# A fused decoder layer: scores ahead of turns in TensorE's order

## What is computed

```python
scores = jnp.einsum('bhsd,bhkd->bhsk', q, k) * scale
probs = jax.nn.softmax(scores, axis=-1)
out = jnp.einsum('bhsk,bhkd->bhsd', probs, v)
```

## Time and profile before

| | before |
|---|---|
| median of three runs | 735.23 us |
| profiled execution | 738.52 us |
| its span, first to last instruction | 736.8 us |
| TensorE matmuls, busy | 636.2 us (86%) |
| ScalarE busy | 415.1 us (56%) |
| VectorE busy | 407.7 us (55%) |
| GpSimd busy | 322.4 us (44%) |
| mean granted TensorE clock | 0.959 |

### The profile page before, as it was taken

The page is one execution under the profiler, slowest core; times in us unless marked ns, Lnnn a source line. Parts: engine busy times, 40 slices in busy tenths (PEclk is TensorE's granted clock), DMA queues, the critical chain, the costliest instruction groups (busy, mean ns, idle before and its releaser), DMA issues.

```text
span 736.8 us, 14686 instructions
## 1 busy us (share of the span) xinstructions
PE 636.2 (86%) x5168; PEld 511.4 (69%) x5168; DVE 407.7 (55%) x1113; ACT 415.1 (56%) x1498; POOL 322.4 (44%) x367
## 2 busy tenths in 40 slices
PE   3465899999999999999999999999998965299893
PEld 1245788887897888788878977887886752255552
DVE  1545555765865585767567655856443424145552
ACT  1222777676776775677667667766765631044441
POOL 4453343464266427444753574263324322234453
PEclk9998899999999999999999999999997995689998
DMA  7210000000000001001000000000000040223330
GB/s 153 65 32 26 1 1 3 22 5 2 1 26 30 1 1 56 1 3 26 29 2 2 1 30 2 1 22 10 1 1 29 30 154 33 92 82 97 96 95 14
DMA packets 25127, 23.60 MB, mean 32 GB/s; under 512 B 7055, under 2 KB 22673, under 8 KB 25056
## 3 DMA queue, kind: packets, MB, share of 16 engines
q1 hardware_dynamic: 21088, 15.83, 7.6%
q0 software_dynamic: 2816, 6.32, 2.4%
q10 hardware_dynamic: 1152, 0.52, 0.6%
HBM read 15.16 MB, written 8.02 MB: 31 GB/s over the span
## 4 chain that ended last, share of the span: by engine, by line
PE 57%; POOL 13%; DVE 9%; issue 8%; ACT 6%; DMA 5%; SPq 1%; POOLq 0%; DVEq 0%
PE bank L1052 7%; PE bank L1082 6%; PE bank L1073 5%; PE bank L1087 5%; PE bank L1062 5%; POOL routed L473 4%; PE bank L1015 4%; PE bank L1160 4%; PE bank L1088 4%; PE bank L1089 4%; ACT prob L863 4%; PE bank L958 2%; POOL prob L481 2%; PE bank L947 2%; DVE mneg L701 2%
## 5 line engine op out<-in xcount | busy, mean ns | idle before, releaser
L863 ACT ACTIVATE prob<-bank,mneg 128x128 f32<-128x128 f32 x512 | 182.5, 380 | 103.8 <-DVE mneg L701 103.8
L481 POOL TENSOR_TENSOR prob<-prob,rden 128x512 f32<-128x512 f32 x128 | 130.7, 1042 | 171.8 <-DVE rden L708 171.8
L863 ACT ACTIVATION_READ_ACCUMULATOR prob<-bank,mneg 128x1 f32 x512 | 111.8, 218 | 0.0
L869 ACT COPY probT<-bank 128x512 f32<-128x512 f32 x128 | 77.6, 606 | 47.7 <-PE bank L1062 46.7
L701 DVE TENSOR_REDUCE mneg<-bank 128x4 f32<-128x512 f32 x128 | 81.3, 678 | 32.1 <-PE bank L1052 32.1
L1052 PE MATMUL bank<-kT,qT 64*128 64x128 f32 x1024 | 76.2, 289 | 11.8 <-ACT kT L879 8.6
L1052 PEld LDWEIGHTS bank<-kT,qT 64*128 64x128 f32 x1024 | 64.0, 191 | 23.5 <-issue 18.0
L1062 PE MATMUL bank<-ident,prob 128*128 128x128 f32 x512 | 78.4, 276 | 0.0
L1073 PE MATMUL bank<-probT,V 128*64 128x128 f32 x1024 | 70.4, 280 | 1.4 <-ACT probT L869 1.4
L1062 PEld LDWEIGHTS bank<-ident,prob 128*128 128x128 f32 x512 | 60.7, 142 | 14.8 <-issue 13.5
L1082 PE MATMUL bank<-xwo,oT 128*128 128x128 f32 x512 | 64.8, 281 | 2.2 <-ACT oT L873 2.2
(11 more groups left out here) (165 smaller groups left out, 1335.2 us busy)
## 6 DMA issues: line engine op xcount, KB each, us to landing
prob<-routed SPq DMA_DIRECT2D x40, 128.5 KB, 2.1
xin<-in_x_dram SPq DMA_DIRECT2D x8, 256.0 KB, 3.0
ctx_nat<-in_ctx_dram SPq DMA_DIRECT2D x8, 192.0 KB, 2.5
routed<-blank SPq DMA_DIRECT2D x9, 128.5 KB, 2.2
qT<-in_L_ffn_rt_gate_dram SPq DMA_DIRECT2D x1, 1024.0 KB, 5.3
qT<-in_L_ffn_rt_up_dram SPq DMA_DIRECT2D x1, 1024.0 KB, 9.0
out_dram<-probT,prob POOLq DMA_INDIRECT x40
prob<-in_L_xattn_Wq_dram SPq DMA_DIRECT2D x1, 512.0 KB, 11.6
```

The costliest lines, as they stand in the source:

```text
L481: nc.gpsimd.tensor_tensor(view, view, spread(rden[:, m % 2, c * NC:(c + 1) * NC], 2, S), ALU.mult)\
L863: last = nc.scalar.activation(prob[:, m % 2, p * S:(p + 1) * S], bank[c % 2][:, i * S:(i + 1) * S], ACT.Exp, bias=mneg[:, m % 2, p:p + 1], ...
L869: nc.scalar.copy(probT[:, m % 2, c * 512:(c + 1) * 512], made(r1, ("T", m, c))[:])\
```

## The change

In the steps `n` that have both batch `n` and batch `n + 1`, and in the even beats, the next batch's `scores` are issued ahead of this batch's `turn_probs` instead of behind them. That is so in 62 beats (31 steps, two beats each). The odd beats, and the order on all other engines, are as they were; the waits of each piece move with it.

```diff
@@ -1119,10 +1119,11 @@
             pe.wait_ge(consts, CONSTS_FIRST)
             for n in range(FIRST, LAST + 1):
                 for b in range(NC):
+
+                    if b % 2 == 0 and live(n + 1):
+                        scores(n + 1, b // 2)
                     if live(n):
                         turn_probs(n, b)
-                    if b % 2 == 0 and live(n + 1):
-                        scores(n + 1, b // 2)
                     if b % 2 and live(n + 1):
                         make_v(n + 1, b // 2)
                     if qk_of(n, b):
```

## The result

| | before | after |
|---|---|---|
| median beside the first comparison | 735.09 us (4 runs) | 742.9 us (4 runs) |
| profiled execution | 738.52 us | 740.88 us |
| TensorE's wait ahead of the scores | 11.8 us | 23.5 us |
| period of four batches, mid-loop | 68.2 us | 69.0 us |

The ratio is 1.0101 (95% interval 1.0072 to 1.013). A second comparison, with five rounds, gave 742.24 against 736.93 us, ratio 1.0077 (1.005 to 1.0104). So the kernel became slower by 5 to 8 us, and both medians lie inside the range given; the forecast of 744.2 lies 1.3 and 2.0 us above the two medians.

What follows compares the result with a forecast made beforehand. TensorE was taken as the bound. Losses of 3.6 us where it already waits (edge place included) and 5.4 us in covered beats make 9.0 us, moving the median from 735.2 to 744.2 us; range 738 to 750.

Steps and rivals of the forecast that it cites:

- waits of today: Where TensorE already waits for ScalarE before scores, turns no longer fill the wait: seven places lose 0.45 us each, 3.15 us.
- covered beats: Each period's first and third even beats, where turns hide ScalarE's lateness: 0.6 and 0.30 us lost, 5.4 us over six periods.
- the beat behind the sigmoids: ScalarE reloads the exponential's table; its copy of turns comes 0.54 us late, of which 0.3 us reaches the next scores.
- The one on the edge: At 513 us turns just cover ScalarE's exponentials; the scores would start at 513.66 instead of 513.19, losing 0.47 us.
- The fifth beat: Fifth even beat of a period: the 0.45 us lost before the scores comes out of the later wait for `h`.
- Usual beats: Even beats where ScalarE is done before the turns start: same 1.62 us sum, exponentials gain 0.04 us, counted as nothing.
- Only the waits of today pay: Rival: the twelve covered beats' margins of 0.27 to 0.33 us close, so they lose nothing; 739 us, chance 0.13.
- no change: Rival: every delay falls into a later wait, as in the fifth beats; 735.5 us, chance 0.11.
- faster: Rival: earlier scores hasten the row maximum if ScalarE's copy starts under about 0.25 us behind the turns; 732 us, chance 0.05.
- the rival of the clock: Rival: TensorE's longer single waits of 1.4 us also lower its granted clock, costing 5 to 10 us; 751 us, chance 0.13.
- the 3.3 us between profile and median: Profiled execution lies 3.3 us above the runs' median; carried over, so 747.5 us profiled means a median of 744.2.
- the rule that was weighed in the prediction: Changing the tiling mode drains TensorE; one more change in the loop's last four even beats, 0.08 us each, 0.3 us, left out.

Runs made afterwards that it cites:

- the fourth experiment: Scores ahead of turns only in the 13 beats where TensorE already waited ahead of the scores, against the kernel before: 737.65 us, ratio 1.003.
- the second experiment: Scores ahead of turns only in each period's first and third even beats, against the kernel before: 738.83 us, ratio 1.005.
- first experiment: Kernel before with the swap only in 23 even beats where ScalarE is done well before the turns: 734.28 us, ratio 0.9978; again 734.79 us, ratio 0.9994.
- exponentials first: Changed kernel, with ScalarE's exponentials of the next batch ahead of its copy of the turns in even beats: 760.31 us, ratio 1.0326.
- keys on VectorE, old order: Kernel before, with the last copy of the keys of each pair of batches made by VectorE instead of ScalarE: 735.29 us, ratio 1.0001.
- more beats with room: Kernel before with the first experiment's swaps plus halves 5, 6, 55, 57, 59, 61 and, unintended, 54 and 62: 737.62 us, ratio 1.0001.
- room only: Kernel before with scores ahead of turns in 29 beats, as in more beats with room but without halves 54 and 62: 734.04 us, ratio 0.9984.
- chosen version: Kernel before with the last keys' copy on VectorE and the swap only in each period's first, second, fourth, sixth and seventh half: 733.74 us, ratio 0.9972.
- new order, keys on VectorE: Changed kernel, with the last copy of the keys of each pair of batches made by VectorE: 737.73 us, ratio 1.0021.
- all but the sigmoid beat: Changed kernel with the old order in each period's eighth half, where ScalarE reloads the exponential's table: 740.3 us, ratio 1.0064.

## Why the prediction was right

- **The bound and what moves.** Swaps with room cost nothing, swaps without it cost what the turns had covered, and one swap made ScalarE late for the beat behind it. The traces add up. From the scores of half 1 to the product behind half 53, at full granted clock in every profile from 81 to 555 us, the changed kernel took 5.92 us more than the one before (433.34 against 427.42). The parts, each against the same stretch: 1.67 us (waits of today) + 2.76 (covered beats) + 2.34 (the beat behind the sigmoids, 5.92 - 3.58) - 0.92 (beats with room) = 5.85 us. The medians of the whole kernels give 2.2 + 3.4 + 1.9 to 2.6 - 0.6 to 1.2 = 6.3 to 7.6 us against 5 to 8, but each of these terms is uncertain by more than 1 us, and six swapped beats are in none of the parts.
- **Waits of today.** Each was to cost 0.45 us and cost 0.37 to 0.41 in the places up to 542 us, measured from the row ahead of the two pieces to the product behind them. Turns between the other pieces hold TensorE 0.41 us, not 0.45, and ScalarE's exponentials start 2.27 us behind the scores, not 2.36, since its instructions overlap by 0.1. The first three beats cost 1.16 us instead of 1.35: by the trace the scores of half 5 start 0.71 us later against those of half 0, and they should start 0.45 sooner. The last two places, at 557 and 578 us, cost 0.57 and 0.60: there `prob_v` stands behind the turns (last section). The one on the edge, at 513 us, cost 0.40 (forecast 0.47).
- **The fifth beat.** Given back at `h`, as worked out; shown by the fourth experiment.
- **The covered beats.** The third cost 0.33 us (forecast 0.30), the first 0.69 to 0.70 (0.6), of which the sigmoid beat's lateness made 0.44. Both terms were a little small.
- **Usual beats.** I had counted them as nothing; each saves 0.02 to 0.08 us, 0.2 in a period. The period grew by 0.8 us, since the covered beats took 1.0 and these gave 0.2 back: the forecast of 0.9 is that close partly because two errors cancel.
- **The rivals.** "Only the waits of today pay" fell with the second experiment, "no change" with the period, "faster" with the copy at 0.69 us behind the turns. The granted clock stayed at full from 77 to 610 us in the profile of the changed kernel, with waits of 1.40 us in it, and in its second profile too, so the rival of the clock is not borne out there.
- **Profile against median.** Here the mechanism had a hole. The forecast took the stretch at the lower clock around 565 us as unchanged, and put the profiled execution at 747.5 us; it took 740.9. Neither profile of the changed kernel has that stretch. From the product behind half 53 to that behind half 63 the kernel before took 78.8 us; the kernel with only the covered beats swapped, which has the old order there and was granted the full clock, took 74.6; the changed kernel took 76.2. So at equal clock the changed kernel is 5.9 + 1.6 = 7.5 us longer, and against the profile of before only 5.9 - 2.6 = 3.3 us. The two medians' differences, 7.8 and 5.3 us, lie between these or next to them; what share of the runs without a profile has the stretch is not known. That the median came within 2 us of 744.2, while the profiled execution missed by 6.6, is partly luck: I had carried the 3.3 us between profile and median without a reason.

## What to carry to other kernels

On an engine with one stream, a ready piece in front of one that must wait fills the wait, and behind it waits too; list for each place the margin between the releaser's end and the new start, and swap only where it is positive. An edit on the full engine can also make a half-idle one late: here two thirds of the worst place's loss came from ScalarE getting its turns too late one beat earlier. And where a delay meets a later wait for something independent it is given back, so add the terms per stretch between such waits.

## What the runs showed of the hardware

The joints between pieces on TensorE have prices that depend on the neighbours. The last even beat, before and after:

```profile
584.38 0.60 PE L1062 MATMUL bank<-ident,prob 128*128 128x128 f32 x4
...
586.01 1.09 PE L1073 MATMUL bank<-probT,V 128*64 128x128 f32 x16
```

```profile
587.39 1.16 PE L1052 MATMUL bank<-kT,qT 64*128 64x128 f32 x16
588.48 0.66 PE L1062 MATMUL bank<-ident,prob 128*128 128x128 f32 x4
589.07 1.09 PE L1073 MATMUL bank<-probT,V 128*64 128x128 f32 x16
```

Here products of half width (L1073) follow. Before, the pair of pieces takes 586.01 - 584.38 = 1.63 us up to them; after, 589.07 - 587.39 = 1.68. The joint ahead of the pair is dearer too: the scores start 1.95 us behind the start of the output product (L1082), the turns started 1.86 behind it. That makes 0.14 us more in this beat, where usual beats save 0.02 or more. The turns are followed after 0.59 us, not 0.41, in all of the last four even beats, so these cost some 4 x 0.18 = 0.7 us more than the same swap elsewhere. That is the direction of the rule that was weighed in the prediction, on "TensorEngine Tiling (Array Packing)" of the Trainium skill: the new order has one more change of tiling mode in these beats. The size had been put at 0.08 us a beat, 0.3 us in all, and left out of the sum. That the change of mode is the cause, and not the other product behind the turns, is not shown.

The granted clock differs between two executions of one program. The windows view from 555 to 575 us (busy us and count of PE, PEld, DVE, ACT and POOL, then the granted clock) of the first experiment's kernel, and of the same kernel profiled again:

```profile
555.00:575.00 20.00, 17.21 (x166) 14.13 (x166) 10.30 (x31) 11.48 (x47) 8.50 (x10) 0.91 0.05 18
```

```profile
555.00:575.00 20.00, 16.54 (x118) 13.86 (x117) 6.88 (x20) 9.68 (x41) 8.31 (x10) 0.74 0.08 28
```

The same wait for `h` stands in this stretch in both:

```profile
559.46 1.11 PE L947 MATMUL bank<-ident,h 128*128 128x128 f32 x4 [1.94 <-DVE h L648]
```

```profile
561.46 0.66 PE L947 MATMUL bank<-ident,h 128*128 128x128 f32 x4 [1.93 <-DVE h L648]
```

In the first, the turn of `h` behind the wait already takes 1.11 us, and the clock is back at full from 565 us on; in the second it still takes 0.66, and the granted clock is 0.50 from 565 to 570 us. From half 53 to half 63 the first took 75.4 us and the second 79.1, so this costs 3.7 us. All profiles together (the clock is that of 555 to 575 us; in the kernel with the exponentials first, whose loop is longer, of 575 to 610 us):

| kernel | wait for `h` | granted clock |
|---|---|---|
| before | 1.94 us | 0.74 |
| first experiment, twice | 1.94, 1.93 us | 0.91, 0.74 |
| keys on VectorE, old order | 2.37 us | 0.74 |
| more beats with room | 2.02 us | 0.74 |
| room only | 2.02 us | 0.91 |
| chosen version | 2.37 us | 0.91 |
| only the covered beats | 1.94 us | 1.00 |
| new order, keys on VectorE | 1.84 us | 1.00 |
| changed kernel, twice; all but the sigmoid beat | 1.44 us | 1.00 |
| only the waits of today | 1.35 us | 1.00 |
| exponentials first | 1.30 us | 1.00 |

So 1.94 us went with 0.74, 0.91 and 1.00, and no profile with a wait of 1.84 us or less has the fall. The changed kernel's wait is shorter since its scores ahead of it come later, and both of its profiles were spared; with so few profiles that is a hint and not a cause shown. A profile with such a stretch can't be laid beside one without it. Whether the runs without a profile have it can't be seen from their times.
